# Seven normalizations of a two-layer hybrid model: epsilon, root and rows on GpSimd

## What is computed

```python
xn = layernorm(x)                                   # "prep"
att = layernorm(attention(xn) + xn)                 # "wo": 16 heads and relative positions, epsilon 0
att = layernorm(ff(att) + att)                      # "ff", epsilon 0
cell = layernorm(six_attention_nodes(xn)) * g + b   # "end": 8 heads a node
x = x + att + cell
u = layernorm(x)                                    # "n0"
h = u + mamba(layernorm(u))                         # "n1": a scan over 16 states
m = h + gelu(layernorm(h) @ W1 + b1) @ W2 + b2      # "n2"
x = x + m + u + mixture_of_2_of_8_experts(layernorm(u))
```

## Time and profile before

| | us |
|---|---|
| median of 3 runs | 1923.71 |
| lowest, highest | 1911.75, 1929.69 |
| the profiled execution | 1941.77 |
| its span, first to last instruction | 1939.9 |
| busy: TensorE matmuls, VectorE, ScalarE, GpSimd | 1325.9, 1217.9, 787.9, 443.2 |

### The profile page before, as it was taken

The page is one execution under the profiler, slowest core; times in us unless marked ns, Lnnn a source line. Parts: engine busy times, 40 slices in busy tenths (PEclk is TensorE's granted clock), DMA queues, the critical chain, the costliest instruction groups (busy, mean ns, idle before and its releaser), DMA issues.

```text
span 1939.9 us, 25490 instructions
## 1 busy us (share of the span) xinstructions
PE 1325.9 (68%) x8542; PEld 846.7 (44%) x8542; DVE 1217.9 (63%) x2380; ACT 787.9 (41%) x1684; POOL 443.2 (23%) x399
## 2 busy tenths in 40 slices
PE   6453677477768687867866776867786786567527
PEld 5221334233556345633654355525563465335416
DVE  4221334379647975597748964896569763876574
ACT  0222334254535454354535453545445452433322
POOL 4002001313140322232221313031303222221060
PEclk8556668676878688977878788868896787668759
DMA  3227223521362224612181137123442125111201
GB/s 130 33 23 73 35 26 39 57 50 17 40 75 74 33 28 51 109 22 29 30 116 42 17 39 99 50 33 37 56 95 33 18 33 94 42 17 28 68 1 57
DMA packets 151439, 94.52 MB, mean 49 GB/s; under 512 B 43104, under 2 KB 133232, under 8 KB 151184
## 3 DMA queue, kind: packets, MB, share of 16 engines
q1 hardware_dynamic: 151312, 92.90, 31.6%
HBM read 44.88 MB, written 3.42 MB: 25 GB/s over the span
## 4 chain that ended last, share of the span: by engine, by line
PE 38%; DVE 22%; DMA 14%; SPq 9%; issue 8%; ACT 7%; POOL 2%; POOLq 1%; DVEq 0%; ACTq 0%
DMA qks<-parts_b 9%; PE scores_t L820 6%; PE attn_out L833 6%; DVE hb L1493 5%; PE ps L800 4%; PE px L980 4%; DVE rowmax_B L1342 4%; PE px L992 4%; SPq L584 4%; ACT probs L1086 3%; DVE hb L1488 2%; SPq L608 2%; SPq L609 1%; DVE work L1462 1%; DMA stage_a<-parts_a 1%
## 5 line engine op out<-in xcount | busy, mean ns | idle before, releaser
L1342 DVE TENSOR_REDUCE rowmax_B<-ps 128x2 f32<-128x512 f32 x384 | 259.4, 688 | 273.0 <-PE ps L800 271.2
L1086 ACT ACTIVATE probs<-scores_t 128x512 f32<-128x512 f32 x512 | 284.9, 594 | 107.9 <-PE scores_t L820 105.2
L800 PE MATMUL ps<-qks 96*128 96x256 bf16 x768 | 184.3, 339 | 162.1 <-DMA qks<-parts_b 126.9
L820 PE MATMUL scores_t<-qks 98*128 98x256 bf16 x768 | 175.9, 347 | 42.5 <-ACT probs L1086 24.2
L992 PE MATMUL px<-ze,w_e 128*128 128x256 f32 x512 | 152.7, 434 | 62.5 <-DMA w_e<-in_w_e 56.3
L800 PEld LDWEIGHTS ps<-qks 96*128 96x128 bf16 x768 | 72.0, 113 | 240.7 <-DMA qks<-parts_b 138.8
L1213 ACT ACTIVATE hb<-px 128x512 f32<-128x512 f32 x128 | 76.4, 597 | 227.0 <-PE px L992 225.7
L1493 DVE TENSOR_TENSOR_SCAN hb<-da,hb 128x1024 f32<-128x1024 f32 x64 | 157.2, 2456 | 2.2
L1628 POOL TENSOR_TENSOR parts_b<-rem_b,parts_b 128x256 bf16<-128x256 f32 x96 | 75.6, 793 | 363.2 <-ACT parts_b L1054 362.0
L1579 DVE SCALAR_TENSOR_TENSOR work<-hb,px 128x512 f32<-128x512 f32 x128 | 87.5, 684 | 111.0 <-ACT hb L1213 110.8
L1174 ACT ACTIVATE da<-gate,a_neg 128x255 f32<-128x255 f32 x256 | 108.5, 499 | 78.0 <-DVE hb L1493 70.1
(11 more groups left out here) (277 smaller groups left out, 2398.5 us busy)
## 6 DMA issues: line engine op xcount, KB each, us to landing
qks<-parts_b SPq DMA_DIRECT2D x288, 128.0 KB, 4.9
w_e<-in_w_e SPq DMA_DIRECT2D x128, 256.0 KB, 3.2
stage_a<-parts_a SPq DMA_DIRECT2D x96, 64.0 KB
pos<-t_scr SPq DMA_DIRECT2D x8, 264.0 KB, 16.7
qks<-maxrow_B SPq DMA_DIRECT2D x96, 4.0 KB
probs<-in_b_we_t SPq DMA_DIRECT2D x1, 1280.0 KB, 6.5
x_in<-in_x SPq DMA_DIRECT2D x8, 128.0 KB, 2.2
v_scr<-va_fm SPq DMA_DIRECT2D x8, 128.0 KB, 15.4
```

Source lines behind the costliest of these rows:

```text
L800: mm = pe.matmul(o[:, qc * L:(qc + 1) * L], q(STACK, qc * P, P), k(STACK, 0, L), start=True, stop=True)
L820: mm = pe.matmul(scores_t[unit % 2][:, kc * L:(kc + 1) * L], k(STACK + 2, kc * P, P), q(STACK + 2, 0, L), start=True, stop=True)
L1086: act.activation(probs[:, group % 2, h % 4, :, :].rearrange("p a b -> p (a b)"), scores_t[unit % 2][:, :], ACT.Exp).then_inc(s_exp, 1)
L1342: dve.tensor_reduce(out=top[:, :, h], in_=parts_of(bank(b, ("max", kind, n))), axis=AX, op=ALU.max).then_inc(max_done[kind].of(b), 1)
```

## The change

The epsilon and the rows of all seven normalizations are made by GpSimd. `root` now waits for mean and variance, adds the epsilon itself and takes the power; `apply` moves from VectorE to GpSimd with its instructions and its waits, and `n0_apply`, `n1_apply` and `prep_apply` with it. GpSimd's order gets seven stages a sequence, each at the place that it had on VectorE; the residual, which shared the name `n0_apply`, is now `n0_res` and follows it. The stages that stay keep their order on every engine. The readers of rows wait on new counters (`rows_steps`). `statistics` waits, before it overwrites its tiles, until GpSimd has used those of the sequence before. The start of each sequence stands in a table (`START`) that holds multiples of 18866 as before.

```diff
@@ the stages of the second layer, and when a sequence starts
-LAYER1 = [("n0_stats",), ("n0_root",), ("n0_apply",), ("n1_stats",), ("n1_root",), ("n1_apply",), ("z_t",)]
+LAYER1 = [("n0_stats",), ("n0_root",), ("n0_apply",), ("n0_res",), ("n1_stats",), ("n1_root",), ("n1_apply",), ("z_t",)]
...
-PERIOD = 18866
+START = {
+    "cell": [0, 18866, 37732, 56598, 75464, 94330, 113196, 132062],
...
@@ GpSimd's places
-        "cell": [-13906, -12668, -3990, 1178, 5234, 12170, 18568, 22376, 22626],
+        "cell": [-13906, -13804, -12668, -3990, 1178, 5234, 12170, 18568, 22376, 22544, 22626],
...
-        "raw": [2725, 4444, 5537, 21730, 21928, 22556, 22785],
-        "one": [23063, 23224, 23437, 27653, 30155, 30874, 31485, 32252, 32865, 33475, 34430, 35399, 36555, 37275, 37509],
+        "raw": [2725, 4444, 5537, 21730, 21860, 21928, 22556, 22670, 22785],
+        "one": [23063, 23224, 23254, 23437, 23519, 27653, 30155, 30874, 31485, 32252, 32865, 33475, 34430, 35399, 36555, 37275, 37509, 37629],
@@ VectorE
-            def statistics(b, kind, src, eps):
+            def statistics(b, kind, src):
                 s = norm_steps[kind]
+                past(dve, rows_steps[kind], b - 1, APPLIED)
                 for h in range(HALVES):
                     last = dve.bn_stats(stats[kind][:, h, :], src[:, h, :])
...
                 last.then_inc(s.of(b), 1)
-                dve.wait_ge(*s.at(b, MEAN))
-                dve.tensor_scalar(veps[kind][:, :], mv[kind][:, :, 1], eps, None, ALU.add).then_inc(s.of(b), 1)
-
-            def apply(b, kind, src, dst):
-                dve.wait_ge(*root_done[kind].at(b))
-                for h in range(HALVES):
-                    last = dve.tensor_scalar(dst[:, h, :], src[:, h, :], mv[kind][:, h, 0:1], rstd[kind][:, h:h + 1], ALU.subtract, ALU.mult)
-                last.then_inc(norm_steps[kind].of(b), 1)
@@ GpSimd
             def root(b, kind):
-                pool.wait_ge(*norm_steps[kind].at(b, VEPS))
-                pool.tensor_tensor(rstd[kind][:, :], veps[kind][:, :], half_neg[:, :], ALU.pow).then_inc(root_done[kind].of(b), 1)
+                pool.wait_ge(*norm_steps[kind].at(b, MEAN))
+                pool.tensor_scalar(veps[kind][:, :], mv[kind][:, :, 1], EPSILON[kind], None, ALU.add).then_inc(rows_steps[kind].of(b), 1)
+                pool.wait_ge(*rows_steps[kind].at(b, VEPS))
+                pool.tensor_tensor(rstd[kind][:, :], veps[kind][:, :], half_neg[:, :], ALU.pow).then_inc(rows_steps[kind].of(b), 1)
+
+            def apply(b, kind, src, dst):
+                pool.wait_ge(*rows_steps[kind].at(b, ROOT))
+                for h in range(HALVES):
+                    last = pool.tensor_scalar(dst[:, h, :], src[:, h, :], mv[kind][:, h, 0:1], rstd[kind][:, h:h + 1], ALU.subtract, ALU.mult)
+                last.then_inc(rows_steps[kind].of(b), 1)
```

More of the change, by code:

```diff
@@ L95 @@
               "z_t inproj xc bcdt sp_u sp_z state h_t ffn ffn_t router expert",
-    "vector": "prep_stats prep_apply q1 k1 a1 max post_b post_a end_y end_apply end_x wo_y wo_apply ff_y ff_apply "
-              "n0_stats n0_apply n1_stats n1_apply n2_stats n2_apply inproj conv xc bc sp_u sp_z state y x2 ffn ffn_t ffn_out router rank expert expert_y",
-    "gpsimd": "prep_root xn_bo q2 k2 a2 reorder end_root end_scale wo_root ab_t ff_root att n0_root n1_root n2_root n0_apply conv sp_z state x2",
-}
-PERIOD = 18866
+    "vector": "prep_stats q1 k1 a1 max post_b post_a end_y end_x wo_y ff_y n0_stats n1_stats n2_stats inproj conv xc bc sp_u sp_z state y x2 ffn ffn_t ffn_out router rank expert expert_y",
+    "gpsimd": "prep_root prep_apply xn_bo q2 k2 a2 reorder end_root end_apply end_scale wo_root wo_apply ab_t ff_root ff_apply att "
+              "n0_root n0_apply n0_res n1_root n1_apply n2_root n2_apply conv sp_z state x2",
+}
+START = {
+    "cell": [0, 18866, 37732, 56598, 75464, 94330, 113196, 132062],
+    "side": [0, 18866, 37732, 56598, 75464, 94330, 113196, 132062],
+    "raw": [0, 18866, 37732, 56598, 75464, 94330, 113196, 132062],
+    "one": [0, 18866, 37732, 56598, 75464, 94330, 113196, 132062],
+}
 PLACES = {
@@ L404, in hybrid_layers @@
         eh_t_done = sig("eh_t_done", 2 * EX)
-        STAT, MEAN, VEPS, APPLIED = range(4)
-        norm_steps = {k: sig(f"norm_{k}", 4) for k in KINDS}
+        STAT, MEAN = range(2)
+        EPSILON = {"prep": EPS, "wo": 0.0, "ff": 0.0, "end": EPS_CELL, "n0": EPS, "n1": EPS, "n2": EPS}
+        norm_steps = {k: sig(f"norm_{k}", 2) for k in KINDS}
+        VEPS, ROOT, APPLIED = range(3)
+        rows_steps = {k: sig(f"rows_{k}", 3) for k in KINDS}
         rem = {"q": sig("rem_q", NODES, 1, 2), "k": sig("rem_k", NODES, 1, 2), "a": sig("rem_a", 1)}
@@ L438, in hybrid_layers @@
         eh_done = sig("eh_done", 2 * EX)
-        root_done = {k: sig(f"root_{k}", 1) for k in KINDS}
         xn_bo_done = sig("xn_bo_done", 1)
@@ L729, in prep_t @@
             def prep_t(b):
-                pe.wait_ge(*norm_steps["prep"].at(b, APPLIED))
+                pe.wait_ge(*rows_steps["prep"].at(b, APPLIED))
                 o = take(b, "xn_t")
@@ L1380, in wo_y @@
                 dve.wait_ge(*wo_y_done.at(b))
-                statistics(b, "wo", y_a, 0.0)
+                statistics(b, "wo", y_a)
             def ff_y(b):
@@ L1387, in ff_y @@
                 dve.wait_ge(*ff_y_done.at(b))
-                statistics(b, "ff", y_a, 0.0)
+                statistics(b, "ff", y_a)
             def end_y(b):
@@ L1395, in end_y @@
                 dve.wait_ge(*end_y_done.at(b))
-                statistics(b, "end", y_end, EPS_CELL)
+                statistics(b, "end", y_end)
             def end_x(b):
@@ L1702, in _ @@
             run_stages("gpsimd",
-                       {"prep_root": lambda b: root(b, "prep"), "xn_bo": xn_bias, "q2": lambda b, c: split_last(b, c, "q"),
-                        "k2": lambda b, c: split_last(b, c, "k"), "a2": a2, "reorder": reorder, "end_root": lambda b: root(b, "end"),
-                        "end_scale": end_scale, "wo_root": lambda b: root(b, "wo"), "ab_t": ab_bias_, "ff_root": lambda b: root(b, "ff"), "att": att,
-                        "n0_root": lambda b: root(b, "n0"), "n0_apply": residual, "n1_root": lambda b: root(b, "n1"), "n2_root": lambda b: root(b, "n2"),
+                       {"prep_root": lambda b: root(b, "prep"), "prep_apply": prep_apply, "xn_bo": xn_bias, "q2": lambda b, c: split_last(b, c, "q"),
+                        "k2": lambda b, c: split_last(b, c, "k"), "a2": a2, "reorder": reorder, "end_root": lambda b: root(b, "end"), "end_apply": lambda b: apply(b, "end", y_end, cell),
+                        "end_scale": end_scale, "wo_root": lambda b: root(b, "wo"), "wo_apply": lambda b: apply(b, "wo", y_a, ab), "ab_t": ab_bias_, "ff_root": lambda b: root(b, "ff"), "ff_apply": lambda b: apply(b, "ff", y_a, y_a), "att": att,
+                        "n0_root": lambda b: root(b, "n0"), "n0_apply": n0_apply, "n0_res": residual, "n1_root": lambda b: root(b, "n1"), "n1_apply": n1_apply,
+                        "n2_root": lambda b: root(b, "n2"), "n2_apply": lambda b: apply(b, "n2", x2, h_tm),
                         "conv": conv, "sp_z": dt_x, "state": state, "x2": residual2})
```

76 lines of the change are left out of this document (37 added, 39 removed).

## The result

| | before | after |
|---|---|---|
| median, us | 1925.66 (4 runs; 1911.75 to 1929.69) | 1952.26 (4 runs; 1939.29 to 1953.17) |
| the profiled execution, its span | 1941.77, 1939.9 | 1953.17, 1950.6 |
| busy: VectorE, GpSimd | 1217.9, 443.2 | 1174.7, 544.8 |

The changed kernel takes 1.0136 times as long, interval 1.0095 to 1.0177: some 26 us (18 to 34) slower. The forecast was 1925 us, no change, with a range up to 1943. That was wrong, in the direction of the rival with the other sign, which had got 0.06.

The account below looks back on a forecast made before the run. The chain changes engine every few microseconds; middle transitions are judged by line 893's and `a2`'s starts, with a DMA wait behind. Terms -1.7 + 1.0 + 1.5 + 0.4 + 0.2 = +1.4 us on 1923.71 gave 1925 us, range 1906 to 1943.

Parts of the forecast that it names:

- the rival with the other sign: GpSimd slow at the moved instructions: pair 1.11 us, epsilon 0.70, `a2` 2.4 us late; +25 us, 1949 us; chance 0.06.
- The price: Cost of the moved instructions on GpSimd: a 128-column row instruction 0.37 us, a pair 0.73, the epsilon 0.18.
- A normalization from its mean to its rows: On GpSimd, epsilon, root, rows and hand-overs: 1.85 us against about 1.6 before, 0.24 us worse.
- A middle transition: Between sequences, b = 1 to 6, from `wo` to `a2`: -0.28 us each, -1.7 us for six.
- the 0.52: At `wo` in a transition: TensorE gains 0.52 us because VectorE, freed of the rows, starts the row maxima earlier.
- VectorE's relief: Rival: work taken off VectorE, with lost collisions, counts in full; -42 us, 1882 us; chance 0.06 of passing 1%.
- The first transition: No slack before `a2`, which starts near 347.95 us instead of 346.94: +1.0 us.
- The first `prep`: The very first `prep` normalization: adds 0.24 us, entered as +0.2 in the sum.
- The last transition: Runs nearly alone, with `wo` itself waited for; the expert half behind `n1`'s statistics starts later: +1.5 us.
- The last `n2`: Behind two residual additions on GpSimd; rows come at 1886.64 us instead of 1886.23: +0.4 us.
- New collisions: Rival: a VectorE chain instruction held 0.76 us in each of four normalizations a transition: 24 us, 1948 us; chance 0.04.
- the stretch behind `a2`: After `a2` in a middle transition: a wait for one `qks` transfer of 15.94 us, until 996 us, DMA 92% busy.

Follow-up runs that it names:

- e6: The changed kernel profiled once more, with no edit: 1950.69 us.
- e10: The changed kernel with one extra 4-byte transfer issued by SyncE behind the fourth `stage_a` issue: 1947.29 us, 1.0124 of the kernel before.
- e1: The changed kernel with probe instructions behind its last GpSimd stage, pricing row instruction forms (the price table); no total time given, its middle 1450.8 us.
- e5: The kernel before profiled once more, with no edit: 1920.26 us.
- e9: The kernel before with one extra 4-byte transfer issued by SyncE behind the fourth `stage_a` issue: 1922.11 us, ratio 0.9966.
- e12: The changed kernel with all rows back on VectorE, epsilon and root on GpSimd: 1929.64 us, 1.0015 of the kernel before.
- e8: The kernel before with four idle subtract-multiplies on GpSimd ahead of each `a2`: 1946.88 us, ratio 1.0087.

## Why the prediction was wrong

**The price, the term that failed.** The row instruction was put at 0.37 us, bounds of a pair 0.55 to 1.11; the pair took 1.58, outside the bounds. Two errors are in it, and the price table separates them. The fixed part of 0.18 us came from instructions on two tensors and is about 0.35 for this form: multiply-add at 128 columns takes 0.45, not 0.37. And the row it was taken from (`cv`) multiplies and adds, while the moved instruction subtracts and multiplies: 0.45 against 0.80. "The same form with two pointer scalars" had looked at shape and operands and not at the operations. The epsilon (0.18, measured 0.23) and the root (0.70, measured 0.72) were right. A normalization from its mean to its rows takes 2.74 us instead of 1.85: 0.89 more.

The Trainium skill (GPSIMD Engine Reference, Engine selection) calls one-input elementwise work on GpSimd roughly line-rate. The runs don't bear this out for the form moved here: 0.80 us for 128x128, where VectorE takes 0.57 to 0.59 for two of them.

**The steps with that price.** The prediction's own sum, with 0.89 added wherever a normalization stands on the path, gives 6 x 2.9 + 3.7 + 5.1 + 1.3 + 1.1 = 28.6 us, where the medians differ by 26.6:

- **A middle transition.** Forecast -0.28. Three normalizations add 2.67, and the rows of `wo`, now on the path, take back the 0.52 that TensorE should have gained: +2.9. Measured +2.9 in the one of b = 3 (19.34 against 16.45), and +2.7 in the mean of the six over four profiles of each (after, e6, e10, e1 against before, e5, e9, e12: 20.0 against 17.3). `att` came 2.9 us later against the mean of `wo` (968.55 - 955.03 against 959.45 - 948.86), forecast 0.7.
  "Alike to within a few tenths of a microsecond" holds for five of the six in the profile of before (17.3 to 17.5 behind `wo`); in the sixth `a2` stands at 18.8.
- **What `a2` is worth.** That the six transitions are judged by `a2` held where it was tried, in e8. The middle, which holds these six and the first transition, grew by 15 us (mean of after, e6, e10 and e1, 1447, against before, e5, e9 and e12, 1432; e12 stands for before, since it has all rows on VectorE). Six times 2.7 is 16 us, and the first transition should have added 3.7 by the steps, so 5 us of the steps are not in it. VectorE's relief of 43 us is not to be seen there.
- **The first transition.** Forecast +1.0, with the price +3.7. Behind `wo` its `a2` stands at 15.05 us before and 19.14 after, +4.1; in e5 it stands at 17.50, so that before itself varies by more than half of it. **The first `prep`**, +0.2 or +1.1 with the price, can't be seen: the first `wo` comes at 331.9 and 326.6 us before, at 327.9 and 326.4 after.
- **The last transition.** Forecast +1.5, with four times 0.89 it is +5.1. (The rival had counted three there, +4.3, though `wo` is on that path too.) Measured +6.1: the expert half of the earlier trace rows starts 14.24 us behind `wo` before, 20.33 after. VectorE waits for it, kernel after:

```profile
1791.44 0.43 DVE L1395 TENSOR_TENSOR x<-x_in,x 128x256 f32<-128x256 f32 x1 [5.04 <-POOL x_in L1661]
...
1795.70 0.49 DVE L1301 BATCH_NORM_STATS2 stats_n<-u 128x6 f32<-128x128 f32 x2 [2.91 <-POOL u L1608]
...
1796.49 0.65 DVE L1564 SCALAR_TENSOR_TENSOR work<-hb,px 128x512 f32<-128x512 f32 x1
```

- **The last `n2`.** Forecast +0.4, with the price +1.3. Measured +1.2: from the end of the last residual addition to the end of the rows 1.85 was forecast, 2.69 measured (1894.76 to 1897.45). Timeline of GpSimd and TensorE, kernel after; before it is the earlier trace rows:

```profile
1894.04 0.72 POOL L1706 TENSOR_TENSOR res<-res,rows 128x256 f32<-128x256 f32 x1
1894.74 0.23 POOL L1601 TENSOR_SCALAR veps_n<-mv_n 128x2 f32<-128x2 f32 x1
1895.05 0.72 POOL L1603 TENSOR_TENSOR rstd_n<-veps_n,half_neg 128x2 f32<-128x2 f32 x1
1895.87 1.58 POOL L1608 TENSOR_SCALAR z_tm<-u,mv_n,rstd_n 128x128 f32<-128x128 f32 x2
...
1897.51 0.69 PE L957 MATMUL px<-ident,z_tm 128*128 128x128 f32 x2 [4.81 <-POOL z_tm L1608]
```

These two make up the tail: 174.5 us in the mean of the same four profiles after, 166.7 before, +7.8. Middle and tail together are +23 us, inside the interval of 18 to 34.

**The rival.** "GpSimd is slow at it" had the place, the mechanism and the size (0.90 a normalization, `a2` 2.4 us late, 1949 us). It came to that by an epsilon at its upper bound, 0.70, and a pair at 1.11; measured they are 0.23 and 1.58, and that the sum is the same is luck. Its chance of 0.06 was an error of its own: it asked for both upper bounds at once, and those came from the wrong row. The text held the point from which it decides (0.3 us dearer in all), and a row price that no trace showed should have carried more than 6 in 100 beyond it. The range, too, was narrower than its own words: -2 and +5 with 17 us either side of 1923.71 are 1905 and 1946, not 1906 and 1943, and the upper price bound of +25 lay outside it. 1952.26 is outside either.

**The other rivals.** VectorE's relief was real (43 us) and no gain from it shows. New collisions were not tried by themselves, but the traces bound them: the 2212 instructions that VectorE keeps take 1251.1 us after and 1245.5 before (count times mean, summed over all groups), 5.6 us more in the whole execution, where the rival needed 24 on the chain. Half of it is one group, a line of before and the same one after:

```profile
L1350 DVE TENSOR_SCALAR negmax_B<-rowmax_B 128x8 bf16<-128x8 f32 x96 | 23.4, 243 | 3.3
...
L1344 DVE TENSOR_SCALAR negmax_B<-rowmax_B 128x8 bf16<-128x8 f32 x96 | 26.4, 275 | 3.3
```

Nor is it TensorE's clock: the granted clock was 0.788 in the mean of the four runs after, and 0.784 to 0.785 in the mean of the runs of before on each of the four chips of the experiments.

**What was missing.** The prediction took the stretch behind `a2` as a transfer of fixed length. It isn't: it varies between 11.5 and 17.6 us over the profiles (b = 1 to 5), with the same transfers and their twelve issues spread over 7.3 to 8.2 us, and in the kernel with only `end`, `ff` and `n0` on GpSimd short transfers go with a late `a2` that costs nothing. That they are what hides it is the reading that fits (e8, with transfers of 15.6 us, pays for a late `a2`), not one that an edit has shown. In the full change it did not vary (16.2 and 16.0 before, 15.8 and 16.1 after), so the miss doesn't come from it. Why the transfers run at one pace or the other stays open: chance from one profile to the next, one more issue, and the moment of `a2` alone do not explain it, and no single part of the change was found that does.
